# One gather for the expert slots' weights and destinations, in a fused two-layer attention and mixture-of-experts kernel

## The reference, cut to what matters

```python
x = x + _L0_xattn_ref(_layernorm(x), ctx_1024, ctx_1024, ...)
# _L0_ffn_ref on layernorm(x), 2048 rows:
scores = softmax(x_flat @ gate_w.T)            # 8 experts
_, topk_ids = top_k(scores, 2)
w = scores * one_hot(topk_ids, 8).sum(axis=1)
g, u = halves of einsum('nh,eih->nei', x_flat, experts_gate_up)   # 352 each
out = einsum('neh,ne->nh', einsum('nei,ehi->neh', silu(g) * u, experts_down), w)
shared = silu(x_flat @ shared_gate_w.T) * (x_flat @ shared_up_w.T) @ shared_down_w.T
out = out + sigmoid(x_flat @ shared_expert_gate_w.T) * shared
x = x + out
x = x + _L1_xattn_ref(...)
x = x + _L1_ffn_ref(...)
```

## Time and profile before

| | us |
|---|---|
| median of 3 runs | 564.47 |
| fastest, slowest run | 563.24, 567.54 |
| the profiled execution, whole | 567.54 |
| the profiled execution, span of the trace | 565.8 |

### The profile page before, as it was taken

How to read it: one execution, slowest core, us unless ns; L and a number is a source line. 1 busy time by engine, 2 the same in 40 slices (tenths; PEclk the granted TensorE clock), 3 DMA queues, 4 the chain that set the end, 5 groups by cost and what they waited for, 6 DMA issues and landing times. The chain is left out here.

```text
span 565.8 us, 9556 instructions
## 1 busy us (share of the span) xinstructions
PE 491.9 (87%) x3126; PEld 396.3 (70%) x3126; DVE 295.8 (52%) x671; ACT 193.2 (34%) x426; POOL 215.0 (38%) x291
## 2 busy tenths in 40 slices
PE   4799997489999999898999999999168899898587
PEld 3566765267787777577999999999145666666466
DVE  4578878452063122314555555555154688976483
ACT  2445544075440022002332333333022545542153
POOL 3210140143333567227975533333153335410075
PEclk9999999859999999998999999999655999998799
DMA  8998000120000223999123322220091000000013
GB/s 303 398 396 187 1 1 1 32 54 0 2 1 30 80 86 112 310 327 266 39 67 103 103 79 76 77 64 31 28 312 61 1 2 1 1 1 1 0 39 112
DMA packets 48352, 53.52 MB, mean 95 GB/s; under 512 B 14737, under 2 KB 42706, under 8 KB 48050
## 3 DMA queue, kind: packets, MB, share of 16 engines
q1 hardware_dynamic: 33794, 22.49, 14.7%
q0 software_dynamic: 7152, 19.67, 10.4%
q10 hardware_dynamic: 7360, 10.75, 6.2%
HBM read 35.78 MB, written 17.12 MB: 93 GB/s over the span
## 5 line engine op out<-in xcount | busy, mean ns | idle before, releaser
L130 POOL TENSOR_TENSOR rstd<-var,mhalf 128x2 f32<-128x2 f32 x32 | 22.5, 704 | 143.1 <-DVE var L123 143.1
L426 DVE TENSOR_REDUCE mx<-banks 128x16 f32<-128x1024 f32 x32 | 39.2, 1224 | 36.1 <-PE banks L287 35.8
L1133 PE MATMUL banks<-w_hi,xgT_hi 128*128 x156 | 55.3, 355 | 1.3 <-ACT xgT_hi L821 1.1
L980 ACT ACTIVATE hg<-banks 128x352 f32<-128x352 f32 x39 | 18.1, 463 | 104.9 <-PE banks L1137 95.0
L1299 DVE TENSOR_TENSOR hgT_lo<-banks,hgT_hi 128x256 fp32r<-128x256 f32 x78 | 24.1, 350 | 56.7 <-ACT hgT_hi L987 56.7
L287 PE MATMUL banks<-kvb,qT 64*128 64x256 f32 x256 | 38.2, 419 | 17.3 <-ACT qT L373 6.6
L1134 PE MATMUL banks<-wd,xgT_hi 128*128 x156 | 50.8, 327 | 0.0
L1070 PE MATMUL banks<-sdn,big 128*128 128x256 f32 x192 | 47.6, 394 | 0.0
L287 PEld LDWEIGHTS banks<-kvb,qT 64*128 64x128 f32 x256 | 23.4, 194 | 31.3 <-issue 12.6
L141 ACT ACTIVATE xn<-x,shift,rstd 128x256 f32<-128x256 f32 (+1 forms) x64 | 34.6, 592 | 28.0 <-POOL shift L132 25.9
L1070 PEld LDWEIGHTS banks<-sdn,big 128*128 128x128 f32 x192 | 34.0, 189 | 12.8 <-issue 9.3
(11 more groups left out here) (216 smaller groups left out, 1107.6 us busy)
## 6 DMA issues: line engine op xcount, KB each, us to landing
w_hi<-in_egu POOLq DMA_DIRECT2D x2, 2816.0 KB, 21.2
expert_rows_in<-zeros SPq DMA_DIRECT2D x1, 5304.0 KB, 42.0
xn<-expert_rows_in SPq DMA_DIRECT2D x39, 128.0 KB, 2.0
y_all<-choices_out SPq DMA_DIRECT2D x16, 256.0 KB, 5.2
wd<-in_egu ACTq DMA_DIRECT2D x8, 352.0 KB, 10.4
wd<-in_egu ACTq DMA_DIRECT2D x4, 704.0 KB, 10.6
out_x<-fo SPq DMA_DIRECT2D x8, 256.0 KB, 2.2
x<-in_x ACTq DMA_DIRECT2D x2, 768.0 KB, 10.3
```

The lines of the kernel that those rows point to most:

```text
L426: nc.vector.tensor_reduce(mx, heads(psS), AX.X, ALU.max).then_inc(max_done.sem, 1)
L1133: nc.tensor.matmul(to, xgT_hi[:, c, k, :], hi, start=(k == 0), stop=False)
```

## The change

The destination column is no longer written for each slot. `zeros` gets 4096 + p (p the partition) in column 257, so that the one zero-filling transfer writes it into every block, the same 128 numbers in each; `nowhere`, its transfer and the wait for it go. The 39 transfers of two columns go out of `fetch`; in their place one transfer brings both columns of all 39 blocks, 4992 pieces of 8 bytes, into `slot_w`. It stands on the SP queue behind the fetches of blocks 0 to 3 and before that of block 4. DVE waits for it behind the last product of the shared expert, ahead of `make_w_lo(v, 0)`, and makes the destinations of all blocks with two instructions on 128 x 39 elements: where the number is 4096 or more, 128 times the block's number is added, and the sum is written as an integer. POOL waits for that before it makes the low parts of expert 2, and its scatter loop has neither the copy nor the wait for it.

```diff
--- before.py
+++ after.py
@@ -604,7 +604,6 @@
         sgu_lo = stage_memory(until_shared_ends, "sgu_lo", [P, 2, KD, SI], F32R)
         sgu = big[:, 3072:3072 + 2 * KD * SI].rearrange("p (w k n) -> p w k n", w=2, k=KD)
         zeros = stage_memory(until_attention_ends, "zeros", [P, DX])
-        nowhere = stage_memory(until_attention_ends, "nowhere", [P, NB])
         kvb = stage_memory(until_attention_ends, "kvb", [P, B * 512 + B * NP * 2 * DH])
         kb = [kvb[:, b * 512:(b + 1) * 512].rearrange("p (h n) -> p h n", h=KD) for b in range(B)]
         vb = [kvb[:, B * 512 + b * 256:B * 512 + (b + 1) * 256].rearrange("p (j n) -> p j n", j=NP) for b in range(B)]
@@ -635,7 +634,8 @@
 
             @block.vector
             def _(dve):
-                nc.vector.memset(zeros[:, :], 0.0).then_inc(zero_made, 1)
+                nc.vector.memset(zeros[:, 0:D + 1], 0.0).then_inc(zero_made, 1)
+                nc.vector.memset(zeros[:, D + 2:DX], 0.0).then_inc(zero_made, 1)
                 nc.vector.memset(gw[:, :, :], 0.0).then_inc(made, 1)
                 nc.vector.memset(mem["ones_row"][:, :], 1.0).then_inc(made, 1)
                 nc.vector.memset(mem["mhalf"][:, :], -0.5).then_inc(made, 1)
@@ -647,7 +647,7 @@
 
             @block.gpsimd
             def _(pool):
-                nc.gpsimd.iota(nowhere[:, :], [[P, NB]], base=ROWS, channel_multiplier=1,
+                nc.gpsimd.iota(zeros[:, D + 1:D + 2], [[1, 1]], base=ROWS, channel_multiplier=1,
                                allow_small_or_imprecise_dtypes=True).then_inc(zero_made, 1)
                 nc.gpsimd.memset(mem["ident"][:, :], 0.0).then_inc(made, 1)
                 nc.gpsimd.memset(mem["head_of_all"][:, :], 1.0).then_inc(made, 1)
@@ -673,13 +673,10 @@
             sp.dma_start(sgu[:, 1, :, :], split(sup_in)).then_inc(shared_in, 16)
             sp.dma_start(sdn[:, 0:5, :], split(sdown_in[0:5 * P, :])).then_inc(shared_in, 16)
             sp.dma_start(sdn[0:SR[5], 5, :], sdown_in[5 * P:SI, :]).then_inc(shared_in, 16)
-            sp.wait_ge(zero_made, 2)
+            sp.wait_ge(zero_made, 3)
             sp.dma_start(xg_dram.rearrange("(c p) d -> p c d", p=P), 
                          zeros[:, :].unsqueeze(1).to_broadcast([P, NB, DX])).then_inc(rows_zeroed, 16)
             sp.wait_ge(rows_zeroed, 16)
-            sp.dma_start(xg_dram.rearrange("(c p) d -> p c d", p=P)[:, :, D + 1:D + 2], nowhere[:, :].unsqueeze(2),
-                         allow_slow_non_contiguous=True).then_inc(rows_zeroed, 16)
-            sp.wait_ge(rows_zeroed, 32)
 
         def split_shared(n):
 
@@ -751,7 +748,7 @@
             [sem(f"bx_in{c}") for c in range(NX)], sem("bt_ready"), sem("bT_done"), sem("bg_ready"), sem("bu_ready"),
             sem("bsilu"), sem("bh_done"), sem("bht_ready"), sem("bhT_done"), sem("bhL_done"), sem("by_ready"), sem("by_done"),
             [sem(f"by_out{c}") for c in range(2)])
-        w_placed, dest_made = sem("w_placed"), sem("dest_made")
+        w_placed, slot_w_in = sem("w_placed"), sem("slot_w_in")
         slot_w = sb("slot_w", [P, NB, 2])
         dest = sb("dest", [P, NB], I32)
 
@@ -806,10 +803,9 @@
         def fetch(sp, b):
             wait(sp, bt_ready, b - NX + 1)
             sp.dma_start(xg[:, b % NX, :], xg_dram[b * P:(b + 1) * P, 0:D]).then_inc(bx_in[b % NX], 16)
-            sp.dma_start(slot_w[:, b, :], xg_dram[b * P:(b + 1) * P, D:D + 2]).then_inc(bx_in[b % NX], 16)
 
         def transpose_rows(b):
-            nc.tensor.wait_ge(bx_in[b % NX], 32 * (b // NX + 1))
+            nc.tensor.wait_ge(bx_in[b % NX], 16 * (b // NX + 1))
             wait(nc.tensor, bL_done, b)
             for k in range(KD):
                 last = nc.tensor.transpose(psum[0][:, k * P:(k + 1) * P], xg[:, b % NX, k * P:(k + 1) * P], mem["ident"][:, :])
@@ -840,6 +836,8 @@
                 sp.wait_ge(scattered, 16 * 2 * NT)
                 for b in range(NX):
                     fetch(sp, b)
+                by_slot = xg_dram.rearrange("(c p) d -> p c d", p=P)
+                sp.dma_start(slot_w[:, :, :], by_slot[:, :, D:D + 2], allow_slow_non_contiguous=True).then_inc(slot_w_in, 16)
                 for b in range(NX, NB):
                     fetch(sp, b)
 
@@ -876,7 +874,7 @@
                     if n + 6 < NU:
                         ln.rstd(pool, (n + 6) // 2, n % 2)
                 pool.wait_ge(routed, 1)
-                pool.wait_ge(rows_zeroed, 32)
+                pool.wait_ge(rows_zeroed, 16)
 
                 halves = lambda first, end: [(s, n + 1) for n in range(first, end) for s in (g_ready, u_ready)]
                 products = ([(d_ready, 3), (d_ready, 4)] + halves(2 * KS, 2 * KS + 2) + [(d_ready, n) for n in range(5, 9)]
@@ -895,6 +893,7 @@
                 pool.wait_ge(h2_done, 2 * KS)
                 load_d(pool, 0, 5, 0, d_hi_in[0])
                 pool.wait_ge(w_hi_in, 16 * KD)
+                pool.wait_ge(routed, 2)
                 pool.wait_ge(lo_made, 2)
                 for e in range(2, E):
                     if e == 2 or W_GROUP[e] > W_GROUP[e - 1]:
@@ -913,9 +912,7 @@
 
                 for b in range(NB):
                     pool.wait_ge(by_done, b + 1)
-                    nc.gpsimd.tensor_copy(dest[:, b:b + 1], slot_w[:, b, 1:2]).then_inc(dest_made, 1)
                     wait(pool, by_out[b % 2], 16 * (b // 2))
-                    pool.wait_ge(dest_made, b + 1)
                     pool.indirect_dma_start(yt_dram[:, :], bass.IndirectOffsetOnAxis(ap=dest[:, b:b + 1], axis=0), yy(b), None,
                                             bounds_check=ROWS + NB * P - 1).then_inc(by_out[b % 2], 16)
                 for c in range(2):
@@ -1271,6 +1268,11 @@
                 add(1)
                 for n in range(2 * KS + 2, 4 * KS):
                     hidden(n)
+                dve.wait_ge(slot_w_in, 16)
+                spread = hot["key"][:, :, :].rearrange("p t e -> p (t e)")[:, 0:NB]
+                v.scalar_tensor_tensor(spread, slot_w[:, :, 1], float(ROWS), blk[:, 0:NB], ALU.is_ge, ALU.mult).then_inc(masked, 1)
+                dve.wait_ge(masked, 2)
+                v.scalar_tensor_tensor(dest[:, :], spread, float(P), slot_w[:, :, 1], ALU.mult, ALU.add).then_inc(routed, 1)
                 dve.wait_ge(w_hi_in, 16 * KD)
                 dve.wait_ge(w_in[0], 16 * KD)
                 make_w_lo(v, 0)
```

## The result

The change makes the kernel slower, as predicted: 587.05 us (585.18 to 587.85, four runs) against 563.86 (562.48 to 567.54), a ratio of 1.0396 with a 95% interval of 1.0339 to 1.0453. Predicted were 589.6 us and a range of 574 to 603. The profiled execution took 591.86 us, with a span of 589.9 and a mean granted clock of 0.927.

The account below looks back on a forecast made before the run. PE was taken to bound the kernel. Down(3) late 25.8, low clock 2.5, less 1.4 idle PE, 0.8 clock dip and 1.0 tail, gave +25.1 us on the 564.5 median: 589.6 us, range 574 to 603.

Parts of the forecast that it names:

- PE sets the pace, DVE has 7.4 us of margin and no more: End of shared expert and expert loop: PE is the path; DVE runs about 7.4 us ahead of down(3).
- landing time T: When the gather lands, which DVE waits for: 262.8, some 31 us after its issue.
- 1.6 us each: Time for each step of 128 pieces on SP's queue beside the weight loads; the gather is 39 such steps.
- to 257: When the weight-load traffic ends; from 242.3 until then the gather gets 9.2 of its 39 steps.
- The other 29.8 run alone, 5.8 us: Gather's remaining steps after the traffic, at 0.195 us a step: 5.8 us.
- Down(3) 25.8 us late: End of shared expert: down(3) starts at 265.8, 3.0 us after the gather's landing, against 239.99.
- I take 2.5: Loss in down(3) from the low clock after idle PE: 2.5 us, between bounds of 1.7 and 10.7.
- Given back 1.43 and 0.8: Before make_d_lo: DVE's wait for expert 0's down weights goes, saving 1.43 us of idle PE and 0.8 of clock dip.
- Gain 1.0: Behind the last block: POOL's cast and idle time between DVE's last product and the scatter go, saving 1.0 us.
- A: Gather gets through the traffic in half the time, landing at about 250; down(3) 13 us late; 576 us; chance 0.16.
- B: Gather runs as if alone, landing at 241.6; down(3) 4.6 us late; 568 us; chance 0.06.
- D: Not slower: gather lands by 234.9, within DVE's margin; 2.1 us gained at PE, 1.0 at the tail; 561.4; chance 0.03.

Follow-up runs that it names:

- e1: Changed kernel with DVE's wait and two instructions moved into the loop before the second block's product, POOL's wait before its scatter loop: 594.88 us.
- c2: The changed kernel without any edit, profiled again: 584.24 us, ratio 1.0396.
- second pair: The kernel before and the changed kernel, both without edit, profiled again in one job (c1 and c2): ratio 1.0396.
- c1: The kernel before without any edit, profiled again: median 563.63 us over 17 runs.
- e6: Kernel before with POOL's copy of each block's destinations made by DVE ahead of its product: 562.9 us, ratio 1.0016.
- e10: Changed kernel with a transfer of 4992 pieces of 4 bytes, into a column nothing reads, and its wait put back: 584.51 us, ratio 1.0399.
- e2: Changed kernel with the gather issued ahead of the fetches of blocks 0 to 3: 570.69 us, ratio 1.0041.
- e11: Changed kernel, gather ahead of four fetches, DVE waiting before block 1's product, its instructions before block 10's, POOL's wait before its scatter loop: 581.23 us.

## Why the prediction was right, point by point

The step "PE sets the pace, DVE has 7.4 us of margin and no more" was right. `down(3)` waits for `x L1214`, DVE for the gather, and in e1, where the wait is elsewhere, `down(3)` is not late.

The landing time T was predicted at 262.8, 31 us after the issue. It was 260.9 in the first profile and 254.7 in the second. The mechanism held and its sizes did not, and that the first result came within 2.6 us of the forecast of 589.6 is in part luck:

- "1.6 us each", the step of 128 pieces beside the loads: from 240 to 250 it was 128 / 115 = 1.1 us. I had read the step from landings. Counted by pieces in the kernel before, from 240 to 248, SP's queue moved 812, so a step was 1.26 us even there, beside loads of 2.1 KB a piece in place of 1.8. With other neighbours the rate was another: 101 pieces a microsecond in the kernel before, 115 in c2, and 182 in the first profile from 252 to 257, where POOL's queue had no work.
- "to 257", the end of the traffic: in c2 the loads were all but through at 251, since ACT's last early load was issued at 239.3 and not at 242.6. With 15 us of traffic I had 9.2 steps in it; measured from 240 to 251 were some (1148 + 141) / 128 = 10. Shorter time and faster steps left the count as it was.
- "The other 29.8 run alone, 5.8 us": 3650 pieces, 28.5 steps, in the 3 us from 251 to 254, by which the gather was all but through. 0.11 us a step, not 0.195. `nowhere` ran alone too, and as fast: its packets number 2361 in the 2 us from 52 to 54, 0.11 us a step. The last of them ran before 58, and the landing came at 61.0; the rest of its 9.4 us had no pieces in it, and dividing all of it by 39 was the error.
- In the profile with the stall the same sum came out by another way. ACT's loads began at 231.3, so 1535 pieces of SP's queue ran from 234 to 236 against 199 of ACT's. After that the two went at one rate (from 252 to 257 912 and 910), and the traffic lasted beyond the gather's end, so no part ran alone. Its T came within 2 us of the forecast by errors that cancelled.

"Down(3) 25.8 us late": 19.2 on the second pair, 23.8 on the first. This is the term that was mis-sized, by T; the 3.0 us from T to `down(3)` measured 263.77 - 260.87 = 2.9.

"I take 2.5" for the low clock: 2.4 and 2.0. PE was idle for 20 to 22 us, not 27; the bound of 10.7 was far off.

"Given back 1.43 and 0.8": `make_d_lo` has no wait in either profile, and the 1.43 us of idle PE is gone. Of the clock's dip nothing came back on the second pair, because c1 has none there: its granted clock is 1.00 in every window from 250 to 270. The dip of the earlier trace rows is not a fixed item of the kernel before. In the first pair it is there before and gone after, with a granted clock of 1.00 in every window from 278 to 300.

"Gain 1.0" at the tail: 0.3. Between DVE's last product and the scatter lie 417.70 - 416.91 = 0.79 us in c2 and 397.10 - 396.00 = 1.10 in c1. The idle 0.84 between cast and scatter that I took for the wait on the cast is there without a cast, too, in e6; so it seems to belong to the start of the indirect transfer and not to the cast. "Nothing waited: 0 us" for `nowhere` was right (e10).

The sum for the second pair: late by 19.2, longer by 2.0, and at the tail 0.3 back. c1's idle PE at the first low products (1.57 us) is gone, while its 1.12 at the third block's (ACT's copy) became 1.54, so 1.15 come back. That makes 19.2 + 2.0 - 1.15 - 0.3 = 19.8, against 20.6 at SP's read (426.90 - 406.34); the 0.8 between them lie somewhere in the loop and were not followed up. So the forecast of +25.1 was 4 us over the second pair and 2 over the first (23.2 in the medians). On the second pair T alone was 25.8 - 19.2 = 6.6 too long, and the clock 0.5; against that stand 1.8 us of gains that didn't come and 1.4 us not followed up, the 0.8 above and 0.6 behind SP's read.

The rivals: A needed turns of several pieces for the gather beside single ones of its neighbours; the counts 1148, 1147 and 1150 show none of that. The Trainium skill (page "DMA: Bandwidth & Descriptors", section "Queues, rings and completion order") has a typical packet of 9 to 17 descriptors for each queue's turn. Packets of one length on all queues would give equal counts as well, but hardly counts that agree to one in each half microsecond, when each of the 16 DMA engines moves only some 3 to 5 pieces of a queue. Only in the first 2 us of the loads in the stalled profile did the gather get more (1535 to 199), and why is open. B and D needed a gather beside no traffic. That was real in e2, where T - issue was 4.7 us, half of the 9.4 of B's bound; there the time was within the noise that of the kernel before, so the lone transfer's length was overrated too, and D was nearer than I put it: a few microseconds between the issue of the gather and the first loads decide it, 1.5 behind it in e2 and 5.0 ahead of it in e11.

## What to carry to other kernels

Many tiny pieces are cheap on empty queues (about 0.6 ns each here, 4992 in some 3 us, landed 4.7 us after the issue) and dear beside large loads, where the gather moved only as many pieces as each of its neighbours, and landed after 24 to 29 us. Joining 39 small hidden transfers into one saves nothing if the joined one is waited for by an engine on the path: keep its first consumer's part small and make the destinations where both DVE and POOL have slack. And before a wait is taken away, read what lands next: here the down weights of expert 0 took the whole gain until their load was split.

## What the hardware showed that was not expected

- DVE's instruction with its operands in SBUF was held for 25.36 us by a row of POOL's instructions (e1), and took 0.18 to 0.20 us where POOL was idle (c2, e11).
- Queues with work move equal numbers of pieces: 1147, 1150 and 1148 in 10 us in c2, 1446, 1448 and 1446 in 13 us in e11, with 8-byte pieces beside ones of 1 to 2 KB. The exception is the start of the loads in the first profile, 1535 to 199 in 2 us.
- An indirect transfer on POOL starts some 0.8 us after what it waited for: DVE's product (0.79 in c2, 0.84 in e6) or, before the change, POOL's own copy (0.84).
- A stall of all engines near 222 us, its releaser "remote", stood in five of fourteen profiles and was absent from the same program profiled again. Its cause is open.
